# Expanding the high levels' table on VectorE in place of GpSimd in a log-linear attention and expert kernel

## The reference

```python
x = x + attn(layernorm(x))
x = x + experts(layernorm(x))

# attn, 8 heads of 128
q, k, v = x @ Wq.T, x @ Wk.T, x @ Wv.T
G = cumsum(-softplus(x @ Wg.T + bg))               # log decay per head
lam = softplus(x @ Wdl.T + Lparam)                 # one weight per head and level (12)
lvl[t, s] = 0 if t == s else floor(log2(t - s)) + 1
A[t, s] = (q[t] . k[s]) * scale * exp(G[t] - G[s]) * lam[t, lvl[t, s]]   # s <= t
out = layernorm(A @ v @ Wo.T + x) * ln_g + ln_b
```

## Time and profile before

| what | value |
|---|---|
| median of 3 runs | 1608.88 us (1608.41 to 1609.42) |
| the profiled execution | 1608.22 us, its span 1606.1 us |
| mean granted clock of TensorE | 0.968 |
| busy: PE, DVE, ACT, POOL | 1456.4, 1030.0, 1141.3, 1143.1 us |

### The profile page before, as it was taken

How to read it: one execution, slowest core, us unless ns; L and a number is a source line. 1 busy time by engine, 2 the same in 40 slices (tenths; PEclk the granted TensorE clock), 3 DMA queues, 4 the chain that set the end, 5 groups by cost and what they waited for, 6 DMA issues and landing times.

```text
span 1606.1 us, 29807 instructions
## 1 busy us (share of the span) xinstructions
PE 1456.4 (91%) x10678; PEld 1210.6 (75%) x10678; DVE 1030.0 (64%) x2466; ACT 1141.3 (71%) x3299; POOL 1143.1 (71%) x1067
## 2 busy tenths in 40 slices
PE   5799997899989999899989999899998999989975
PEld 5588886778867887777877788678786887878853
DVE  5457565676657766586655866467674676647665
ACT  2689886786768767686766967678676886867631
POOL 1486779766896678956798667975679666896570
PEclk8799999999999999999999999999999999999987
DMA  5200100010100101001010010001010000100000
GB/s 176 64 18 16 39 28 15 10 37 20 36 15 7 38 22 36 13 15 42 10 35 13 25 36 20 23 16 35 23 36 12 10 26 19 36 16 28 8 8 13
DMA packets 80332, 44.01 MB, mean 27 GB/s; under 512 B 21832, under 2 KB 78522, under 8 KB 80058
## 3 DMA queue, kind: packets, MB, share of 16 engines
q1 hardware_dynamic: 79484, 41.83, 9.2%
q10 hardware_dynamic: 702, 0.29, 0.1%
HBM read 32.39 MB, written 9.18 MB: 26 GB/s over the span
## 4 chain that ended last, share of the span: by engine, by line
PE 55%; POOL 18%; DVE 12%; ACT 9%; issue 4%; DMA 1%; ACTq 0%; SPq 0%; POOLq 0%; DVEq 0%
PE o_ps L1320 15%; PE l_ps L1251 7%; PE s_ps L1235 6%; POOL a_lo L596 6%; PE s_ps L1237 6%; PE s_ps L1236 6%; PE aux L1235 4%; ACT w_all L714 4%; PE aux L1236 4%; PE aux L1237 4%; DVE a_all L912 2%; ACT a_hi L737 2%; POOL ra L581 2%; POOL e_rs L602 1%; POOL yx L441 1%
## 5 line engine op out<-in xcount | busy, mean ns | idle before, releaser
L596 POOL TENSOR_TENSOR a_lo<-a_all,a_hi 128x512 fp32r<-128x512 f32 (+2 forms) x640 | 709.1, 1125 | 323.9 <-ACT a_hi L737 322.7
L912 DVE TENSOR_TENSOR a_all<-s_ps,w_all 128x512 f32<-128x512 f32 (+3 forms) x768 | 422.6, 554 | 488.4 <-PE s_ps L1237 476.3
L714 ACT ACTIVATE w_all<-l_ps,bias 128x128 f32<-128x128 f32 x2304 | 628.5, 386 | 58.1 <-PE l_ps L1251 57.5
L737 ACT ACTIVATE a_hi<-a_all 128x512 fp32r<-128x512 f32 (+2 forms) x640 | 364.0, 591 | 254.8 <-DVE a_all L912 251.5
L1320 PE MATMUL o_ps<-a_hi,v_all 128*128 128x512 f32 (+2 forms) x1280 | 472.1, 373 | 56.9 <-POOL a_lo L596 56.8
L1320 PEld LDWEIGHTS o_ps<-a_hi,v_all 128*128 128x128 f32 x1280 | 243.9, 191 | 110.5 <-POOL a_lo L596 72.5
L1235 PE MATMUL s_ps<-q_hi,xt_hi 128*128 128x512 f32 (+3 forms) x768 | 290.4, 378 | 2.5 <-DVE a_all L912 2.5
L1236 PE MATMUL s_ps<-q_lo,xt_hi 128*128 128x512 f32 (+3 forms) x768 | 268.3, 349 | 0.0
L1237 PE MATMUL s_ps<-q_hi,xt_lo 128*128 128x512 f32 (+3 forms) x768 | 268.0, 349 | 0.0
L1320 PE MATMUL o_ps<-a_lo,v_all 128*128 128x512 f32 (+2 forms) x640 | 232.4, 363 | 0.0
L1237 PEld LDWEIGHTS s_ps<-q_hi,xt_lo 128*128 128x128 f32 x768 | 147.0, 191 | 17.1
(11 more groups left out here) (175 smaller groups left out, 2216.1 us busy)
## 6 DMA issues: line engine op xcount, KB each, us to landing
mt<-m_scratch SPq DMA_DIRECT2D x62, 128.0 KB, 2.0
nt<-n_scratch SPq DMA_DIRECT2D x62, 128.0 KB, 2.6
tx<-in_L_attn_x SPq DMA_DIRECT2D x9, 512.0 KB, 4.1
out<-yn SPq DMA_DIRECT2D x16, 256.0 KB, 2.3
yx<-in_L_attn_x SPq DMA_DIRECT2D x7, 512.0 KB, 4.2
ea<-ea_scratch SPq DMA_DIRECT2D x126, 16.0 KB, 1.9
eb<-eb_scratch SPq DMA_DIRECT2D x126, 6.0 KB, 1.8
ea_scratch<-tx SPq DMA_DIRECT2D x15, 128.0 KB
```

The source lines that it names most:

```text
L596: pool.tensor_tensor(a_lo[r][:, 0:t1 - t0], a[r][:, 0:t1 - t0], a_hi[r][:, 0:t1 - t0].bitcast(F32), ALU.subtract).then_inc(a_lo_done, 1)
L714: last = act.activation(w[k][:, W_AT[j] + dd, :].rearrange("p (f c) -> p f c", f=2), l_ps[:, :, slot * HF:(slot + 1) * HF], ACT.Exp, bias= ...
L737: act.activation(a_hi[r][:, 0:t1 - t0], a[r][:, 0:t1 - t0], ACT.Copy).then_inc(a_hi_done, 1)
L912: dve.tensor_tensor(a[(n * NG + g) % NA][:, 0:t1 - t0], s_ps[:, g % 2, 0:t1 - t0], w[n % 2][:, at:at + (t1 - t0) // P, :].rearrange("p i n ...
```

## The change

`rb` is computed by DVE in place of POOL, with the same operands. DVE waits for the landing of the small tables (`e_in`) and for the units that still read the buffer (`l_mm`), which POOL's `expand_a` did for both. In the loop it stands at the same place 21 of each head; ahead of the loop the first two stand behind `take_q(0, .)`. SP waits for `ra_ready` besides `rb_ready` ahead of a load, since two engines now read the small tables.

```diff
@@ sync: load_e(n)
                     if n >= 2:
                         sp.wait_ge(rb_ready, n - 1)
+                        sp.wait_ge(ra_ready, n - 1)
@@ gpsimd
-                def expand_b(n):
-                    k = n % 2
-                    pool.tensor_tensor(rb[k][:, :, :, :].rearrange("p i n q -> p (i n) q"),
-                                       eb[k][:, :, None].broadcast_to([KB, NC * NTB, TB]),
-                                       c("dmb", KB)[:, None, :].broadcast_to([KB, NC * NTB, TB]),
-                                       ALU.mult).then_inc(rb_ready, 1)
@@
                 for n in range(2):
                     expand_a(n)
-                    expand_b(n)
@@
-                        if place == EXPAND_B and n + 2 < NH:
-                            expand_b(n + 2)
@@ vector
+                def expand_b(n):
+                    k = n % 2
+                    dve.wait_ge(e_in[k], E_IN * (n // 2 + 1))
+                    if n >= 2:
+                        dve.wait_ge(l_mm, NU * (n - 1))
+                    dve.tensor_tensor(rb[k][:, :, :, :].rearrange("p i n q -> p (i n) q"),
+                                      eb[k][:, :, None].broadcast_to([KB, NC * NTB, TB]),
+                                      c("dmb", KB)[:, None, :].broadcast_to([KB, NC * NTB, TB]),
+                                      ALU.mult).then_inc(rb_ready, 1)
@@
                 for u in range(Q_U):
                     take_q(0, u)
+                for n in range(2):
+                    expand_b(n)
                 dve.wait_ge(s_we, 16)
@@
+                        if place == EXPAND_B and n + 2 < NH:
+                            expand_b(n + 2)
```

## The result

The kernel after has a median of 1679.26 us (1677.59 to 1679.52, 4 runs), against 1608.64 us of the kernel before on the same chip: a ratio of 1.0436, with a 95% interval of 1.0418 to 1.0454. It is slower by 70.6 us, where 14 us had been forecast.

What follows compares the result with a forecast made beforehand. PE bounds the kernel, busy 1456.4 of 1606.1 us with 55% of the chain, POOL next with 18%. Terms 5.5 + 4.9 - 3.4 + 7.0 = +14.0 us on 1608.2 led to 1622.5 us, range 1611 to 1630.

Steps and rivals of the forecast that it cites:

- Head h = 1: Heads h = 1, batches 1 to 7: `rb` gets in behind POOL's `a_lo`, PE's later waits go; -3.4 us.
- Head h = 2: Heads h = 2, seven batches: `rb` on DVE costs PE 1.0 us each, nothing won back; +7.0 us.
- rival C: DVE can't get between POOL's instructions in h = 1 and 2: +25 to +35 us more, 1650 us; 7 in 100.
- The sum: Start, normal heads, h = 1 and h = 2 add to +14.0 us on 1608.2: 1622.2, given as 1622.5.
- the start: Ahead of the loop, two expansions on DVE meet POOL's `ra` and delay L1195 by 4.9 to 6.1 us; +5.5 us.
- the normal heads: Place 21 of other heads: `rb` waits for `a_lo`; h = 0 loses 0.55 us in seven batches; +4.9 us together.
- The price of the operation: `rb` on DVE takes 1.22 us without a meeting, reading for about 1.07; POOL stands still about 1.0 us.
- the forecast's second: At the start, DVE first: second `rb` waits for the first `ra`, ends at 46.7 us; L1195 4.9 us late.
- Rival A: Faster: the two engines don't block each other in this form; -7.9, 1601 us; chance 7 in 100.
- rival D: The forecast within the bounds of its terms for start and heads: 1612 to 1630 us; chance 78 in 100.

Runs made afterwards that it cites:

- the form that never waits: Kernel after with `rb`'s second input read from PSUM, a maximum in place of the product, ahead of `q_lo`: 1609.76 us, ratio 1.0012.
- the last version: Kernel before with `rb` of h = 1 (batches 1 to 7) on DVE at place 47, no extra row: 1605.46 us, ratio 0.9972.

## Why the prediction was wrong

**The failed step** is the one in "Head h = 1" (and by the same reasoning "Head h = 2"): "`rb` gets in there", that is behind the one row that POOL is running. In batch 2 it was passed over at eight boundaries in h = 1 and at four in h = 2, and over batches 1 to 7 these heads cost 23.8 and 40.8 us in place of -3.4 and +7.0. It was rival C's mechanism, with a chance of 7 in 100, and its sign came: `rb` shows 11.0 to 11.3 us in h = 1. Putting POOL back in these heads brought 63 us, making POOL stand still 54 us, a short row 54 us. The sum also had no term for TensorE's clock: 24.4 of the 64.6 us in these heads are PE's longer busy time at a lower one.

**Why I believed it.** The earlier trace rows show a DVE instruction that ends when the POOL row ends. I read from this that a boundary is enough. In both places no row stood behind the boundary: POOL was idle there for 1.81 us (507 us) and 0.68 us (138 us). The forecast took the same for the start and the normal heads, and there it held, but mostly without a test: in 35 of the 48 POOL had no row behind, in one it came to `tx`. In the other twelve an `a_lo` followed without a gap and `rb` still went first, as in h = 4 of batch 2 (1.71 us). ACT's `a_hi`, which that row needs, was ready only at 554.05 us, while the row ahead of it had begun at 553.85; in all twelve it came 0.04 to 0.45 us after that begin. The `a_lo` rows that passed `rb` in h = 1 and 2 had had their `a_hi` for 4.2 us and more when the row ahead began. That this is the difference is what the traces suggest, no run took it by itself, and it doesn't tell why a short row opens the way.

**Rival C's size.** It had 25 to 35 us; the runs show 63. It let `rb` wait till POOL runs out near 462 us, "3 to 5 us of new wait per batch". h = 1 cost 3.4 us a batch, 1.7 of it PE's longer busy time; in batch 2 the new wait was the 3.16 us shown. It left out what h = 2 costs, where behind `rb` stood not only a `weigh` but `z`, with 5.8 to 7.0 us a batch. "A request 0.3 us ahead of POOL's next start is short" was no reason: with 0.36 us it was kept out, and with 0.40 us it was kept out where POOL only had a wait that was met, and let in where it had a short row.

**The price of the operation** was right: 1.21 us without a meeting (h = 3 of batch 0; 1.22 forecast), a mean of 1206 ns in the form that never waits, and 1.3 to 2.3 us in the normal heads (1.6 to 2.3 forecast). That POOL pays about 1.0 us and not the whole instruction is borne out by the `tx` rows (0.98 in the last version).

**The start** was +4.2 us, 5.5 forecast. The order was the forecast's second, DVE first, for which it had L1195 4.9 us late. That instruction (L1198 after) stood at 49.08 in place of 45.08, 4.0 late. Mis-sized was the time at which it begins: the tables were there at 42.01, not 42.62. The meeting with the second `ra` was as forecast: the second of the weights' instructions began at 47.26 and ended when POOL's `ra` did, at 47.9.

**The normal heads**: h = 0 lost 0.41 to 0.44 us in six of seven batches (0.55 forecast) and 0.74 in batch 3. The step was right: there PE's wait for ACT's exponentials went from 0.27 us to 0.69. In batch 0 h = 0 and h = 6 cost 0.25 and 0.26 us and h = 4 nothing (1.0 together forecast); h = 3 came out at -1.4 us over the batches, where I took zero; POOL's `rb` being gone, the row of 1.83 us takes 0.21 there in batch 2. Together with the start this part is 7.4 us by the run with the two heads on POOL, where I had 10.4.

**The prices of h = 1 and h = 2** were near in the case they were made for: -0.69 and +1.18 us in batch 2 with POOL made to give way, -2.3 and +9.4 over the seven batches. That kernel's 1625.15 us stands 2.6 above the forecast. Rival A fell (`rb` is not 1.22 everywhere). Its own condition, no blocking, was met in the loop by the kernel with a PSUM input, and gave 1609.8 us, not 1601: over the eight batches h = 4 and h = 7 lost 4.0 and 4.7 us (up to 1.2 and 0.8 in one), with the instruction at its other place, and the start was still paid, 4.4 us.

**A slip in the range.** The bounds of rival D's terms add up to +5.9 to +22.1 us, 1614 to 1630 us, where the prediction has 1612 to 1630. The result lies far outside either.

## What to carry to other kernels

A DVE instruction that needs what POOL holds didn't simply wait here for the row that POOL was in. Where POOL had a backlog of ready rows with two inputs, it waited for all of them, so read how many of POOL's rows stand back to back behind the place, not how long one is. Where an operation must be moved, look for a place at which POOL comes to a one-input row or has a gap, or give the DVE form a PSUM operand: h = 1 and 2 were then 8.5 us shorter than before over the seven batches, in place of 64.6 longer. Judge such a move head by head: fourteen instructions of 64 made 63 of the 71 us. And look at the granted clock beside the waits: idle time that was added went with a lower one, which made the same products longer.

## What the hardware showed that I had not expected

- Behind ready two-input rows of POOL of 128 elements and more, an instruction of DVE took 10.0 to 12.0 us in h = 1, whether it had 64 or 1024 elements, and whether it had two inputs in SBUF or a single one (10.65 us).
- A two-input row of 64 elements or fewer on POOL let it in (1.50 to 1.55 us), one of 128 did not (11.68), and one-input rows let it in at every size from 8 to 512 (1.50 to 2.00, all in h = 1). Why the size matters stays open.
- A useless instruction of 128x8 on POOL, in two heads of seven batches, made the kernel after 54 us faster.
- An instruction of 8 elements on DVE, there in the kernel before too, took 2.82 us when POOL's row behind the boundary was `rb`, and 0.93 when it was the `a_lo` alone (kernel before, same place). In this kernel POOL's backlog delays DVE's small work as well.
